# Expert stages of a layer on one core: rows turned by another engine, outputs in six banks, high halves and gates on ACT

## The reference, cut to what matters

```python
packed = buf[:E * capacity].reshape(E, capacity, d)          # 16 x 1280 x 256
h = gelu(einsum('ecd,edf->ecf', packed, w1) + b1)            # 256 -> 1024
expert_out = einsum('ecf,efd->ecd', h, w2) + b2              # 1024 -> 256
out = (gathered * w).reshape(tokens, k, d).sum(axis=1)       # times the gate, summed over 2 experts
```

## Time and profile before

| | us |
|---|---|
| median of 3 runs (3318.73 to 3320.21) | 3319.15 |
| the profiled execution, its own time | 3325.69 |
| its span, first to last instruction | 3323.9 |
| first stage of experts | 292 to 1290 |
| second stage of experts | 2306 to 3324 |

### The profile page before, as it was taken

How to read it: one execution, slowest core, us unless ns; L and a number is a source line. 1 busy time by engine, 2 the same in 40 slices (tenths; PEclk the granted TensorE clock), 3 DMA queues, 4 the chain that set the end, 5 groups by cost and what they waited for, 6 DMA issues and landing times. The chain is left out here.

```text
span 3323.9 us, 63196 instructions
## 1 busy us (share of the span) xinstructions
PE 2899.8 (87%) x22656; PEld 2337.1 (70%) x22656; DVE 2005.2 (60%) x4425; ACT 1337.9 (40%) x2281; POOL 1695.3 (51%) x1510
## 2 busy tenths in 40 slices
PE   4453999999999995899999999974999999999997
PEld 4453888888888883466756666664888888888886
DVE  4343555555555653577888888753555555565563
ACT  3341444444444442343444444421444444444442
POOL 2543554554545443356676767644345445454543
PEclk9999999999999997899999999965999999999998
DMA  9813333343333324601111111002333334334334
GB/s 305 285 67 103 75 81 81 74 86 78 76 83 87 77 51 115 208 15 37 35 48 34 47 34 47 27 31 94 78 76 82 81 73 86 84 72 88 81 66 136
DMA packets 231849, 281.02 MB, mean 85 GB/s; under 512 B 18999, under 2 KB 214651, under 8 KB 231520
## 3 DMA queue, kind: packets, MB, share of 16 engines
q1 hardware_dynamic: 173760, 203.16, 20.3%
q0 software_dynamic: 57888, 75.16, 12.9%
HBM read 142.44 MB, written 146.41 MB: 87 GB/s over the span
## 5 line engine op out<-in xcount | busy, mean ns | idle before, releaser
L688 ACT ACTIVATE be_h<-be_pH,b 128x512 f32<-128x512 f32 (+1 forms) x384 | 237.2, 618 | 555.5 <-PE be_pH L623 483.1
L688 ACT ACTIVATE ae_h<-ae_pH,b 128x512 f32<-128x512 f32 (+1 forms) x384 | 237.2, 618 | 539.8 <-PE ae_pH L623 487.8
L714 POOL DMA_INDIRECT acc_a<-ae_ob,ae_to x160 | 254.9, 1593 | 94.1 <-POOL ae_ob L706 66.7
L706 POOL TENSOR_SCALAR ae_ob<-ae_ob,ae_gate 128x256 f32<-128x256 f32 x160 | 174.3, 1191 | 247.5 <-DVE ae_ob L829 247.5
L714 POOL DMA_INDIRECT acc_b<-be_ob,be_to x150 | 238.4, 1589 | 88.2 <-POOL be_ob L706 62.3
L706 POOL TENSOR_SCALAR be_ob<-be_ob,be_gate 128x256 f32<-128x256 f32 x150 | 163.0, 1183 | 222.4 <-DVE be_ob L829 222.4
L1461 POOL TENSOR_TENSOR m_xf<-m_tmp,m_xT 128x512 f32<-128x512 f32 x160 | 181.3, 1159 | 119.3 <-DVE m_tmp L1182 119.1
L434 POOL DMA_INDIRECT slots_a<-ar_row,ar_sidx x128 | 125.9, 984 | 158.7 <-issue 150.3
L1514 POOL DMA_INDIRECT slots_b<-m_row,m_sidx x128 | 152.9, 1195 | 84.0 <-issue 84.0
L1756 PEld LDWEIGHTS m_PP<-m_RP,m_KS 64*64 64x64 f32 x6656 | 121.1, 139 | 88.4 <-issue 87.3
L1756 PE MATMUL m_PP<-m_RP,m_KS 64*64 64x64 f32 x6656 | 135.7, 226 | 37.6 <-DVE m_A L1212 36.5
(11 more groups left out here) (342 smaller groups left out, 9384.7 us busy)
## 6 DMA issues: line engine op xcount, KB each, us to landing
ae_stage<-in_w SPq DMA_DIRECT2D x64, 512.0 KB
be_stage<-in_w SPq DMA_DIRECT2D x64, 512.0 KB
slots_a<-empty SPq DMA_DIRECT2D x10, 2080.0 KB, 19.7
ae_xp<-slots_a SPq DMA_DIRECT2D x80, 260.0 KB
slots_b<-empty SPq DMA_DIRECT2D x10, 2080.0 KB, 19.2
be_xp<-slots_b SPq DMA_DIRECT2D x80, 260.0 KB
ar_xin<-in_x SPq DMA_DIRECT2D x16, 512.0 KB, 5.8
acc_a<-ar_xin SPq DMA_DIRECT2D x16, 512.0 KB
```

The costliest lines, as they stand in the source:

```text
L688: t = act.activation(dst[:, 0:SIZES[b]], pH[c % 2][:, 0:SIZES[b]], ACT.Gelu, bias=S.b1[:, bass.ds(i * (2 * FC) + (u * FC + f), 1)])
L706: t = pool.tensor_scalar(ob[m][:, q, :], ob[m][:, q, :], gate[m][:, q:q + 1], None, ALU.mult)
L714: pool.indirect_dma_start(S.acc[tag][:, :], bass.IndirectOffsetOnAxis(ap=to[m][:, q:q + 1], axis=0), ob[m][:, q, :], None, bounds_check=T ...
```

## The change

Turning: a load now brings a block's rows in strips. Per block, 8 transfers (4 groups of 32 partitions, 2 halves of the channels) put pieces of 32 channels (128 bytes) so that each 32x32 square lies where its transpose belongs; DVE transposes the squares of a unit in one instruction (STREAM_TRANSPOSE, `x32`), and `split_x` goes on from SBUF. `turn` and `pT` are gone. The tails of all rows of an expert (4 floats each) come in one transfer of their own. Banks: `pO` has three homes of two banks, units 0 to 4 in homes 0, 1, 2, 0, 1. ACT makes the high halves of the weights after four given chunks (HIGHS) and multiplies the outputs by their gates at chunks 2 and 3. DVE makes the low halves at four given chunks (LOWS); `split_h` stands ahead of `out`, and the two outputs of a block are taken at chunks 1 and 2. SP's order of loads changes with it.

```diff
-        xp = [sb(f"xp{m}", [P, 2, ROW]) for m in range(UNITS)]
+        xq = [sb(f"xq{b}", [P, DC, SIZES[b]]) for b in range(BLOCKS)]
+        tails = [sb(f"tails{u}", [P, 2 * UNITS, ROW - D]) for u in range(2)]
+        x32 = [sb(f"x32_{r}", [P, DC, BS]) for r in range(2)]
...
-        pO = ps("pO", [P, 4, 2 * D])
+        pO = [ps(f"pO{r}", [P, 2, 2 * D]) for r in range(3)]
+        HOME = (0, 1, 2, 0, 1)
...
+                def load(i, u, b):
+                    m = units(b)[-1]
+                    if due(i * NU + (u - 1) * UNITS + m + 1):
+                        sp.wait_ge(xp_free, i * NU + ((u - 1) * UNITS + m + 1))
+                    e = i * 2 + u
+                    n0, n1 = b * FULL // BLK, (b * FULL + SIZES[b]) // BLK
+                    for j in range(QUADS):
+                        for k in range(DC):
+                            cs = slice(k * P + j * BLK, k * P + j * BLK + BLK)
+                            sp.dma_start(xq[b][j * BLK:(j + 1) * BLK, k, :].rearrange("i (n d) -> i n d", d=BLK),
+                                         x_d[e][:, n0:n1, cs]).then_inc(xq_loaded[b], 16)
...
+                load(0, 0, 0)
                 for k in range(2):
                     weights(0, 0, k)
...
-                            weights(i1, u1, 0)
+                            for k in range(2):
+                                weights(i1, u1, k)
+                            load(i1, u1, 0)
+                            load_tails(i1, u1)
                             bias(i1, u1)
...
+                            for k in range(2, 4):
+                                weights(i1, u1, k)
+                            load(i1, u1, 1)
+                            load(i1, u1, 2)
...
-                def turn(i, u, m):
...
+                HIGHS = [(0, 1), (0, 3), (0, 5), (1, 4)]
...
+                        if f in (2, 3) and not (first and c < FC):
+                            u0, b0, _ = place(c - FC)
+                            for m in units(b0)[f - 2:f - 1]:
+                                if not (END and last and c >= FC and u0 == 1):
+                                    scale(i if c >= FC else i - 1, u0, m)
+                        if (b, f) in HIGHS and not (last and u == 1):
+                            weights_high(i if u == 0 else i + 1, 1 - u, HIGHS.index((b, f)))
...
+                    dve.transpose(x32[n % 2][:, :, :], xq[b][:, :, ts]).then_inc(turned, 1)
                     dve.wait_ge(turned, i * NU + n + 1)
...
-                    dve.tensor_copy(xT[r][HI][:, :, ts], pT[n % 2][:, :, :]).then_inc(xT_high, 1)
+                    dve.tensor_copy(xT[r][HI][:, :, ts], x32[n % 2][:, :, :]).then_inc(xT_high, 1)
...
+                LOWS = [(0, 2), (0, 4), (0, 6), (1, 6)]
...
-                        if f == 1 and not (first and c < FC):
+                        split_h(i, c)
+                        if f in (1, 2) and not (first and c < FC):
                             u0, b0, _ = place(c - FC)
-                            for m in units(b0):
+                            for m in units(b0)[f - 1:f]:
```

More of the change, by code:

```diff
@@ L654, in down @@
                     t.then_inc(chunk_down, 1)
-                for m in units(0):
-                    turn(0, 0, m)
                 def step(i, first, last):
@@ L664, in step @@
                             down(i, c - LAG)
-                        u1, b1, over = after(u, b)
-                        if f in (2, 4) and not (over and last):
-                            j = f // 2 - 1
-                            if j < len(units(b1)):
-                                turn(i + 1 if over else i, u1, units(b1)[j])
                     if last:
@@ L862, in step @@
                                 split_x(i + 1 if over else i, u1, units(b1)[j])
-                        if b < 2 and f in (4, 7) and not (last and u == 1):
-                            weights_low(i if u == 0 else i + 1, 1 - u, 2 * b + f // 7)
+                        if (b, f) in LOWS and not (last and u == 1):
+                            weights_low(i if u == 0 else i + 1, 1 - u, LOWS.index((b, f)))
                     if last:
```

117 lines of the change are left out of this document (49 added, 68 removed).

## The result

The changed kernel takes 3226.08 us (median of 4 runs, 3223.01 to 3228.06), the one before 3319.68 in the same comparison. The ratio is 0.972, with a 95% interval of 0.970 to 0.973: 93.6 us less. The forecast was 3251, with a range of 3215 to 3300.

The account below looks back on a forecast made before the run. The prediction took PE, busy 87% of the span, to bound the kernel. Its terms, -70 - 37 + 4 + 37 + 9 - 3 - 8 = -68 us, gave a median of 3251 us, range 3215 to 3300.

Parts of the forecast that it names:

- rival A: DVE's cast and transpose quicker than assumed, shortening block 2's waits: 20 to 31 us less, 3220 to 3231; chance 0.27.
- Block 2: In the 256-column chunks, longer `split_x` on DVE makes PE wait 1.2 us an expert: +37 us.
- The bound: PE bounds the expert stages: 56.1 us of needed matmuls per expert, 4.9 us of turns and DVE waits reachable.
- The turns: Turns leave PE: 0.44 us each, five for each of 32 experts, all on the path: -70 us.
- POOL's high halves: PE's wait through DVE's `weights_low` for POOL's late high half goes, 1.2 us an expert: -37 us.
- The outputs: Old waits around `out` at chunk 1 go (-45 us), new waits for output banks come (+49): net about +4.
- The strips: Loads in 128-byte pieces raise the DMA share from 0.37 to 0.41 to 0.52; on the path only at stage starts.
- Rival C: Strips choke the DMA queues, deciding from 56 ns a packet; at 64 ns 3434 us; chance 0.04.
- The starts: At each expert stage's start, eight load issues ahead of the first weights cost 4.6 us, twice: +9 us.
- The ends: First stage's end: ACT's quicker multiplication frees POOL, -3 us; second's: chunks split ahead of DVE's merge wait, -8 us.
- Rival B: DVE's transpose slower: gain gone at 1.8 us, 3338 at 2.1 us; chance 0.09, a third of it still faster.
- Rival D: More small waits than seen, such as late ACT or POOL's descriptors against DVE's casts, 1 us an expert: 3283; chance 0.18.

Follow-up runs that it names:

- e10: Kernel before with only the rows loaded in strips and turned on VectorE, SyncE keeping its old order; 3406.00 us, ratio 1.0395 to the kernel before.
- e12: e10 with SyncE issuing weights and rows in the changed kernel's order, weights ahead of rows; 3308.46 us, ratio 1.0097 to the kernel before.
- e5: Kernel before with only ScalarE making the weights' high halves, low halves and weight loads placed as in the changed kernel; 3232.70 us, ratio 0.9870.
- e1: Changed kernel with `out` issued before `split_h` again at chunk 1 of a block, six banks kept; 3195.34 us, ratio 0.9606 to the kernel before.
- e2: Changed kernel with four output banks in two homes instead of six in three, new order kept; 3415.82 us, ratio 1.0265 to the kernel before.
- e6: Changed kernel loading x in one transfer of whole 1024-byte rows per block instead of eight in strips; 3184.36 us, ratio 0.9731 to the kernel before.
- e3: Changed kernel with each transpose done twice, the extra one into an unread spare buffer; 3272.38 us, ratio 0.9836 to the kernel before.
- e7: Changed kernel with the outputs multiplied by their gates on POOL again; 3203.66 us, ratio 0.9790 to the kernel before.

## Why the prediction was right, step by step

The sign, the range and the main mechanism held; the median came 25 us below the forecast, inside what rival A gave (3220 to 3231). Block 2, where rival A put it, is 15 of the 25; that the rest adds up to rival A's figure is luck. Means in this part are by the distance of starts, over the 13 experts named above.

- **The bound.** Right: PE's waits and turns were 4.9 us of an expert's 60.99; 1.7 are left of 57.79. (16 x 2.8 + 8 x 1.4 is 56.0, not 56.1.)
- **The turns, -70.** No run has this term by itself. Taken alone the change of the turning costs time (e10, e12): the waits behind POOL grow. Beside the high halves on ACT the rest pays: the changed kernel is 52 us below e5's level (93.6 less 41.7), and that is turns, banks, gates and block 2 together. By the rows before, a turn took 0.44 us at each of the 63 places where it stands alone in 410 to 1240, so 2.2 us an expert, as said.
- **POOL's high halves, -37.** -41.7 (e5): the wait I took as 1.2 us an expert was 1.36 in the mean. That they carried the turns as well is what I did not see; it is my reading of e10 and e12, since no run has those two parts and nothing else.
- **The outputs, +4.** Of the two new waits the first was forecast at 1.13 and measured 1.07 at 426.02. In every other expert it is longer behind ACT's gap, up to 1.94 at 775.49, so 1.26 in the mean, and with the second (0.29) 1.55 for the 1.5 forecast: right in the quiet experts, and in the sum by luck. The old waits were 1.3 us an expert, not 1.4. Together about +8. e1 shows the 39 us that this order cost; e2 that without the added banks the same order would have cost 183 more.
- **Block 2, +37.** The failed step. I took 0.72 for the cast because the nearest row read PSUM; it took 0.43 to 0.47, and a `split_x` 2.13 us (413.69 to 415.82), not 2.4. PE's waits there came to 0.6 us in a quiet expert and 0.7 in the mean instead of 1.2: 15 us too much. It is rival A's mechanism, and the row that could have told it, a cast from SBUF, was not in the trace; the Trainium skill (VectorE: DVE Perf Modes, Mode 2×_2P) had it, and the trace after agrees: 0.43 us.
- **The strips.** A share of 0.47 within the 0.41 to 0.52 forecast, nothing on the path (e6). Rival C is out by far.
- **The starts, +9.** From the first load to the first up matmul 16.1 us instead of 10.9, and 16.2 instead of 10.9 in the second stage: +5.2 and +5.4.
- **The ends.** Last down matmul to the end of the first stage: 17.0 to 14.9, -2.1 for -3. The second stage gained 8.7 us more than the first, which had 2.1 at its own end: about -11 for -8. The number is near, the mechanism is not: PE's two waits in the last expert, 4.03 and 2.04 us, did not shrink but became

```profile
3187.34 0.79 PE L652 MATMUL be_pO<-be_w,be_hT3h 128*128 128x512 f32 x1 [5.43 <-DVE be_hT3l L818]
...
3205.83 0.50 PE L652 MATMUL be_pO<-be_w,be_hT3h 128*128 128x512 f32 x1 [0.75 <-DVE be_hT3l L818]
```

  6.18 us for 6.07. What went is a third wait, which the prediction did not price (before, then the last 64 us before and after):

```profile
3268.09 0.79 PE L648 MATMUL be_pO<-be_w,be_hT0h 128*128 128x512 f32 x1 [3.78 <-DVE be_ob L829]
```

```profile
3260.00:3324.00 64.00, 40.47 (x196) 33.76 (x194) 20.85 (x41) 15.60 (x30) 13.05 (x13) 0.80 0.32 109
3160.00:3224.00 64.00, 45.02 (x240) 37.94 (x239) 25.52 (x51) 20.10 (x38) 20.67 (x20) 0.90 0.50 173
```

  There `out` of the second unit stood on VectorE behind the first unit's merge, and PE waited for the banks that it empties; after the change no wait on `out` is left in that stretch. The clock rose from 0.80 to 0.90, some 6 us of 64, an estimate from these windows.
- **Rival B** (a transpose over 1.8 us) is out: 0.705 us. Its slope was right (e3). The 311 ns that the prediction took from the Trainium skill (VectorE: DVE Perf Modes, The three transpose paths) stand there for bf16; for float32 the trace's number counts. **Rival D** did not come; e7 shows that with the gates left on POOL most of it would have: +22 us of 32.

The profiled execution before was 6.5 us over its median, and the sum allowed for that; the one after was on its median. Of the 25 us between forecast and median, block 2 is 15, the high halves 5 and the last expert 3; the outputs were 4 the other way, the starts and the first stage's end 3. That makes 16. The other 9 or so are some 0.3 us an expert in distances of starts too small to be put down to a place; their cause is open.

## What to carry to other kernels

When several parts of a change lift the same wait from different sides, price them together: here the turns alone made the kernel 1 to 4% slower and the high halves alone 1.3% faster, the whole change 2.8% faster. When output banks are added, look again at the order of the instructions that fill and empty them: the new order would have cost 183 us more on four banks, and on six moving one line back gave 39 us. When waits are priced, look at the granted clock behind them as well: in e2, e10 and e12 it cost, by the estimates above, tens of microseconds that no wait shows. A moved load takes its place in a queue with all its waits: ask which transfer stands behind it.
